# The first layer of a two-layer recurrent network: rounds of one group in place of one-tile steps

## What is computed

```python
x = L0_attn_x
xn = _layernorm(x, axis=-1)
s = _L0_attn_ref(xn, L0_attn_W, L0_attn_b, L0_attn_ln_w, L0_attn_ln_b)   # gated recurrence over the tokens
g = _silu(_L0_ffn_ref(xn, L0_ffn_W_in, L0_ffn_b_in, L0_ffn_W_out))        # a feed-forward over trees
x = x + s * g
xn = _layernorm(x, axis=-1)
s = _L1_attn_ref(...)      # a delta-rule recurrence with short convolutions
g = _silu(_L1_ffn_ref(...))  # two layers of local attention
x = x + s * g
```

## Time and profile before

| | us |
|---|---|
| median of 3 runs | 1857.45 (1856.72 to 1860.48) |
| the profiled execution | 1856.29, its span 1854.5 |
| layer 0 in that span | about 0 to 761 |
| busy over the span: PE, DVE, ACT, POOL | 1559.4, 1405.7, 1111.0, 1106.3 |

### The profile page before, as it was taken

The page is one execution under the profiler, slowest core; times in us unless marked ns, Lnnn a source line. Parts: engine busy times, 40 slices in busy tenths (PEclk is TensorE's granted clock), DMA queues, the critical chain, the costliest instruction groups (busy, mean ns, idle before and its releaser), DMA issues. The chain is left out here.

```text
span 1854.5 us, 32799 instructions
## 1 busy us (share of the span) xinstructions
PE 1559.4 (84%) x11144; PEld 1143.4 (62%) x11144; DVE 1405.7 (76%) x2637; ACT 1111.0 (60%) x3167; POOL 1106.3 (60%) x1524
## 2 busy tenths in 40 slices
PE   6989898989898876587127999999999999999975
PEld 4667676667667765233014767777776777777753
DVE  2557677777767697279946999999899898889844
ACT  1346565656566665243304777777777777787762
POOL 0346364656465573026638888888888888888800
PEclk9999898989899987698558999999999999999987
DMA  3466464656475774176620111011111111111004
GB/s 93 139 222 221 148 228 137 228 170 224 155 243 176 239 246 144 33 215 189 210 99 19 36 37 21 26 37 37 37 37 37 36 32 35 37 37 29 16 9 139
DMA packets 147820, 206.49 MB, mean 111 GB/s; under 512 B 67779, under 2 KB 100933, under 8 KB 147525
## 3 DMA queue, kind: packets, MB, share of 16 engines
q0 software_dynamic: 36864, 134.76, 21.5%
q1 hardware_dynamic: 105554, 65.40, 13.2%
q10 hardware_dynamic: 5234, 4.23, 0.8%
HBM read 167.13 MB, written 24.64 MB: 103 GB/s over the span
## 5 line engine op out<-in xcount | busy, mean ns | idle before, releaser
L304 POOL DMA_INDIRECT l_rows<-in_table,l_idx x256 | 337.0, 1316 | 284.9 <-DVE l_idx L635 169.7
L437 PE MATMUL l_acc<-l_rows,ident 128*128 128x128 f32 x2048 | 316.6, 312 | 72.5 <-ACT l_rows L531 68.1
L437 PEld LDWEIGHTS l_acc<-l_rows,ident 128*128 128x128 f32 x2048 | 282.7, 219 | 106.7 <-ACT l_rows L531 100.3
L531 ACT ACTIVATE l_rows<-l_rows,l_act 128x128 f32<-128x128 f32 x1024 | 306.1, 387 | 2.1
L1351 ACT ACTIVATE lo_s_ps<-lo_s_ps,lo_nmx,lo_rn 128x128 f32<-128x128 f32 x512 | 223.5, 444 | 9.8 <-DVE lo_nmx L1592 9.4
L585 DVE TENSOR_TENSOR l_rows<-l_rows,xn_tok 128x2048 f32<-128x2048 f32 x64 | 146.0, 2281 | 9.4 <-DMA l_rows<-in_table,l_idx 9.4
L1470 POOL TENSOR_TENSOR lo_de_kS<-lo_de_S,lo_de_ops 128x384 f32<-128x384 f32 x128 | 138.8, 1084 | 22.6 <-DMA lo_de_ops<-scratch_ops 13.7
L586 DVE TENSOR_REDUCE l_dot<-l_rows 128x16 f32<-128x2048 f32 x64 | 146.3, 2286 | 2.2
L522 ACT ACTIVATE l_AT<-l_log,top_bias 128x512 f32<-128x512 f32 (+1 forms) x96 | 63.8, 684 | 130.7 <-PE l_log L395 115.6
L403 PE MATMUL l_S<-top_out,l_AT 128*128 128x144 f32 (+3 forms) x832 | 124.1, 298 | 20.9 <-ACT l_AT L522 15.9
L403 PEld LDWEIGHTS l_S<-top_out,l_AT 128*128 128x128 f32 (+2 forms) x832 | 110.1, 198 | 33.6 <-ACT l_AT L522 20.9
(11 more groups left out here) (268 smaller groups left out, 3938.4 us busy)
## 6 DMA issues: line engine op xcount, KB each, us to landing
lo_VE<-lo_V SPq DMA_DIRECT2D x64, 128.0 KB, 2.7
scratch_ops<-pr_ops SPq DMA_DIRECT2D x4, 1792.0 KB, 6.3
lo_de_ops<-scratch_ops SPq DMA_DIRECT2D x16, 448.0 KB, 4.1
l_rows<-in_table,l_idx POOLq DMA_INDIRECT x256
lo_de_qo<-scratch_qo SPq DMA_DIRECT2D x16, 256.0 KB, 4.6
x_tok<-in_x SPq DMA_DIRECT2D x8, 256.0 KB, 5.1
scratch_q<-pr_stage_q SPq DMA_DIRECT2D x8, 256.0 KB, 3.7
scratch_k<-pr_stage_k SPq DMA_DIRECT2D x8, 256.0 KB, 2.4
```

Source lines behind the costliest of these rows:

```text
L304: pool.indirect_dma_start(rows[L][:, r % SLOTS, p, :], None, a[f"table{L}"], bass.IndirectOffsetOnAxis(ap=at[:, p:p + 1], axis=0)).then_in ...
L437: ins = pe.matmul(out, m["ident"][:], rows[L][:, r % SLOTS, p, (FAN + f) * D:(FAN + f + 1) * D], start=False, stop=(L == 5 and k == PICK - ...
L531: ins = act.activation(z, z, ACT.Copy, scale=actv[L][:, r % 2, k:k + 1])
```

## The change

The loops over one-tile steps are replaced, on each of the four engines, by a loop over rounds g of one group: 12 rounds (10 on POOL). In a round each piece of a group, and each of the four tiles' pieces, is named once, with its own lag in groups, from 0 to 4; so the pieces of up to five groups stand in one round. Their order within the round is written out and is new. `tile_ok` is replaced by `on`, which tells whether a group exists. `norms` takes the round's number. The waits for `middle`, `late` and `padded` move into the pieces that need them first, and the wait for the transposed input stands before the logits 0 and 1, since 1 comes first now. The pieces themselves, their buffers and `POS` are the same. The diff, cut where a pattern repeats:

```diff
-            for r in range(FIRST, LAST):              # POOL
-                if tile_ok(r + 2):
-                    gather(4, r + 2)
-                if grp(r, 1) is not None:
-                    sigmoids(grp(r, 1))
-                if tile_ok(r):
-                    gather(5, r)
-                if grp(r, -2) is not None:
-                    scale(grp(r, -2))
+            for g in range(NG + 2):
+                if on(g - 2):
+                    scale(g - 2)
+                if on(g - 1):
+                    gather(5, GT * (g - 1) + 0)
+                    gather(5, GT * (g - 1) + 1)
+                    gather(4, GT * (g - 1) + 3)
+                if on(g):
+                    gather(4, GT * (g) + 0)
+                if on(g - 1):
+                    gather(5, GT * (g - 1) + 2)
+                if on(g):
+                    gather(4, GT * (g) + 1)
+                    sigmoids(g)
+                if on(g - 1):
+                    gather(5, GT * (g - 1) + 3)
+                if on(g):
+                    gather(4, GT * (g) + 2)
...
             def logits(h, k):
                 n, d = POS[h, k], level_of(k)
-                if k == 0:
+                if h == 0 and k < 2:
+                    pe.wait_ge(middle, 16 * len(MIDDLE0))
+                if k < 2:
                     pe.wait_ge(xT_ready.sem, xT_ready.after(h))
```

More of the change, by code:

```diff
@@ L246, in layer0_phase @@
         ids = lambda ap: ap.rearrange("p j d -> p (j d)")
-        tile_ok = lambda r: 0 <= r < NT
+        on = lambda h: 0 <= h < NG
         grp = lambda r, lead: (r + lead) // GT if (r + lead) % GT == 0 and 0 <= (r + lead) // GT < NG else None
@@ L360, in gate @@
                 q = (1, 3, 0, 2)[n]
+                if (h, n) == (0, 0):
+                    pe.wait_ge(late, 16 * len(LATE0))
                 if 4 * h + n:
@@ L442, in _ @@
             pe.wait_ge(consts.sem, 1)
[L443 to L474, removed]
@@ L488, in keep_m @@
             def keep_m(h):
+                if h == 0:
+                    act.wait_ge(padded.sem, 1)
                 act.wait_ge(m_turned.sem, m_turned.after(h))
@@ L607, in choose @@
             def choose(h, d):
+                if (h, d) == (0, 0):
+                    dve.wait_ge(late, 16 * len(LATE0))
                 if d == 0:
@@ L646, in scan, with norms @@
                 ins.then_inc(c_ready.sem, 1)
-            def norms(hx, hc, hm):
+            def norms(n):
+                hx, hc, hm = (h if on(h) else None for h in (n, n - 3, n - 4))
                 if hm is not None:
@@ L696, in norms @@
                     ins.then_inc(xn1_ready.sem, 1)
[L698 to L714, removed]
+            for g in range(NG + 4):
+                if on(g) or on(g - 4):
+                    norms(g)
+                if on(g - 1):
+                    choose(g - 1, 2)
+                if on(g - 3):
+                    dots(4, GT * (g - 3) + 3)
+                    choose5(GT * (g - 3) + 3)
+                if on(g - 2):
+                    dots(4, GT * (g - 2) + 0)
+                if on(g - 3):
+                    dots(5, GT * (g - 3) + 2)
+                if on(g - 2):
+                    dots(4, GT * (g - 2) + 1)
+                if on(g - 3):
+                    dots(5, GT * (g - 3) + 3)
+                if on(g - 2):
+                    choose5(GT * (g - 2) + 0)
+                    dots(4, GT * (g - 2) + 2)
+                if on(g - 1):
+                    choose(g - 1, 3)
+                if on(g - 2):
+                    choose5(GT * (g - 2) + 1)
+                if on(g):
+                    choose(g, 0)
+                if on(g - 2):
+                    scan(g - 2)
+                    dots(5, GT * (g - 2) + 0)
+                    choose5(GT * (g - 2) + 2)
+                    dots(5, GT * (g - 2) + 1)
+                if on(g):
+                    choose(g, 1)
 def sized(ap):
```

155 lines of the change are left out of this document (130 added, 25 removed).

## The result

The changed kernel took 1804.13 us (1800.04 to 1807.75, four runs) beside 1858.97 us for the kernel before: ratio 0.9703, 95% interval 0.9677 to 0.973. That is 54.8 us less where 118.7 us less was forecast, and 65 us above the predicted time, outside its range.

The account below looks back on a forecast made before the run. Order across engines, not one full engine, bounded layer 0. Filling 182.4, four rounds of 71.4 and drain 173.8 made 641.8 us, 118.7 less, the rest unchanged: 1739 us (forecast band 1726 to 1750, wider range 1715 to 1778).

Parts of the forecast that it names:

- the steady round: One full round of layer 0, a group's period: 68.8 us walked plus 2.6 for the clock, 71.4 against 86.22 before.
- The walk: Layer 0's new order followed piece by piece, each starting when its engine is free and its releaser done: round 68.8 us.
- Rivals (a) to (d): (a) gathers bind, 1764, 0.28; (b) stalls overlap better, 1718, 0.13; (c) PE stands for `gelu_top`, 1859, 0.04; (d) round unshortened, 0.03.
- wrong if the distance is over 78: Sign in layer 0: successive groups' choice 3 over 78 us apart, not 69 to 74; gathers or ACT's `gelu_top` the culprit.
- the tail: End of layer 0, from the start of the last `dots` to the last copy: 22.0 us, kept from the earlier trace.
- the two draining rounds: Rounds 8 and 9 of layer 0, the first without new groups: 64.5 and 60.2 us.
- rival (a): In layer 0's rounds the gathers bind: round 75.6 us, total 1764; chance 0.28, with milder slips of its kind.
- Norms and `scale`: DVE's norms fall from 14.1 to 12.0 us as POOL's `scale` moves beside a `dots`; at worst 2.7 lost a round.
- PE's wait for logits (h,1): In each steady round PE idles 1.7 us until ACT reaches `gelu_top` 11 behind a 5.0 us `gelu`.
- The clock: PE's granted clock in a steady round: 2.6 us lost, the middle of the bounds 0 and 5.2.
- PE and DVE close the round together: End of the walked steady round: both engines allow the next round at about the same time, 68.8 us.
- B: Cause named in the experiments' expectations: DVE's norms, running at the same time, hold back PE's completions; no chance given.

Follow-up runs that it names:

- `c1_after`: The changed kernel with nothing edited, run again in a later session beside the kernel before: 1746.28 us, ratio 0.9408.
- `f1_light`: The changed kernel with every second matmul of the spreads left out (part of the computation missing): 1743.78 us, ratio 0.9395 to the kernel before.
- `e8_stand`: The changed kernel with PE made to wait for three small DMAs in each of six rounds: 1810.11 us, ratio 0.9752 to the kernel before.
- `e12_light`: The changed kernel with every second matmul of the spreads left out, in an earlier session than `f1_light`: 1745.40 us, ratio 0.94 to the kernel before.

## Why the prediction was wrong, and where it was right

**The step that failed** is the steady round. The walk took each piece's completion to reach its waiters at once, and no rival had PE held beyond its own work. In the first timing its completions came late in seven successive rounds and ACT stood 59.1 us for them, where the walk had none of it; the full rounds took 79.4 us in the mean, not 71.4. Rivals (a) to (d) all name other causes. DVE's waits for rows are 7.5 us in the round shown; PE stands 1.6 us ahead of logits for ACT, and its 7.1 us ahead of `weigh` are for an ACT that itself waits for PE; and the round did shorten. The prediction's test "wrong if the distance is over 78" did fire, at 82.4, but neither culprit it named was the one.

**The walk itself held** where nothing comes late. By `c1_after`, term by term: the fourth norms begin at 182.17 (182.4 forecast); four rounds are 287.2 (285.6); round 8 67.4 (64.5); round 9 64.6 (60.2); to the last `dots` 27.5 (27.1); the tail 21.2 (22.0). Layer 0 ends at 650.1, 8.3 late, of which 7.3 are the two draining rounds. There rival (a)'s mechanism shows at small size: DVE waits 4.97 and 2.89 us, then 4.56 and 3.89, for gathered rows where the walk had 3.1 and next to nothing. What follows layer 0 came out 2.4 us longer where 0 was forecast. In sum 1746.3 against 1739.

**Norms and `scale`.** The last four normalizations take 1.10 us, as forecast, and the norms 12.1 us (326.21 to 338.35; 12.0 forecast). `scale` now meets a `dots`. Timelines of DVE, POOL and PE in the kernel after:

```profile
289.82 1.10 DVE L773 TENSOR_SCALAR xn_tok<-x_tok,l_mv,l_rstd 128x128 f32<-128x128 f32 x4
...
323.79 3.45 DVE L673 TENSOR_TENSOR l_rows<-l_rows,xn_tok 128x2048 f32<-128x2048 f32 x1 [4.49 <-DMA l_rows<-in_table,l_idx]
...
323.80 1.28 POOL L314 TENSOR_TENSOR l_n<-l_n,lnw 128x512 f32<-128x512 f32 x1
325.16 3.21 POOL L315 TENSOR_TENSOR l_n<-l_n,lnb 128x512 f32<-128x512 f32 x1
...
329.34 1.04 PE L392 MATMUL l_log<-l_xT,top_in 128*64 128x512 f32 x2 [1.59 <-ACT l_AT L583]
```

The `dots` takes 3.45 us where it took 2.28: it is longer by about POOL's 1.28, and then POOL's second instruction takes 3.21. One waited for the other's whole instruction, in turn. That agrees with the rule of the Trainium skill (SBUF - State Buffer, Who interferes with whom) which the prediction weighed. The loss was less than half of the upper bound, 1.17 us a round and not 2.7, as POOL's second instruction is the one that waits. Rival (a)'s premise shows too: in `c1_after` a gather's first issue at 300.46 takes 2.79 us beside the first half of a `dots` (300.11 to 302.39), where 0.94 is usual, and so did the 2.78 of the earlier trace rows.

**PE's wait for logits (h,1)** is 1.59 us (1.7 forecast). **The clock**: 0.98 in the round of `c1_after`, 1.4 us lost of 71.6 where 2.6 were taken.

**PE and DVE close the round together** was wrong: half of the spreads' matmuls could go for 0.6 us (`f1_light`). DVE and the gathers close it. So the 2.6 us of clock, added on PE's account, came out right by luck: DVE waits 6.6 us a round for rows, where the walk had some 4.

**What stays open** is why PE's completions are late in two sessions of six. Shown: whether they come goes with the session and not with the kernel's text; ACT's waits for them hardly grow with the transfers; a made pause takes their place in its own round. More than one cause fits, and they were not separated. One is that PE is held for working too densely (W), which fits that the kernel before moves by 3 us only (PE's busy share in its round is 0.88 against 0.94 in `c1_after`). Another is POOL's row of issues beside PE's work (A), which fits the releases 1.5 to 2.0 us behind that row and DVE's waits for itself. The kernels with less of PE's work and those with the row of issues broken up fell only into sessions where there was nothing to remove, so both are argued, not shown; B was not tested at all. Whether it is the chip, its surroundings or the hour wasn't separable either: two sessions on chips of the same number came out on either side, and I can't say that it was the same chip.

## What to carry to other kernels

Take the new kernel unedited into every session of experiments as a control: four edits looked like cures until it gave the same time. Where nothing came late, a walk through the releases forecast a steady round within 0.5 us and the filling within 0.3; the first is in part luck, as said above. The draining rounds, where gathers follow each other with less work between, need their own landings counted. If an order crosses engines, change it on all of them: without the new order of POOL, which mostly issues transfers, 17 us were left of the 110.

## What the hardware showed that I had not expected

The same program took 1746 or 1806 us depending on the session, while another program with the same work on PE, spread over 86 us a round instead of 72, moved by 3 us between the same sessions. Where it is slow, completions of PE reach their waiters 6 to 8 us after the modelled end of the matmuls, mostly 1.5 to 2.0 us after the last of eight gather issues in a row, and DVE stands up to 0.8 us for its own instructions (1.2 beside more transfers). PE has no record meanwhile, and the granted clock is 0.5 behind it (two blocks of `weigh` take 4.21 us; at full clock, in `e8_stand`, they took 2.23). Six pauses of some 10 us made on purpose at that place cost only 3.3 us in all there. And PE with less to do is granted a lower clock, 0.90 in `e12_light` against 0.98, without any loss of time.
